# Building the head stacks of two attention layers on the chip, without a copy in DRAM

## The reference, cut to what matters

```python
x = x + tanh(g_xattn[0]) * L0_xattn(layernorm(x), ctx)     # X: 8 heads of 64
x = x + tanh(g_ffn[0])   * L0_ffn(layernorm(x))            # F: 16 heads of 8, and experts
x = x + tanh(g_xattn[1]) * L1_xattn(layernorm(x), ctx)     # B (keys and values: K): 16 heads of 8
x = x + tanh(g_ffn[1])   * L1_ffn(layernorm(x))            # C: experts
# in F and B, for each head:
attn = einsum('bhqd,bhkd->bhqk', q, k) / sqrt(8)
out  = einsum('bhqk,bhkd->bqhd', softmax(attn), v)
```

## Time and profile before

| what | value |
|---|---|
| median of 3 runs | 926.0 us (921.73 to 927.47) |
| profiled execution, span | 931.0 us; the profile gives no time around it |
| PE busy | 764.6 us, 82% of the span |
| DVE / ACT / POOL busy | 634.9 / 353.3 / 299.8 us |
| mean granted clock of PE | 0.861 of full speed |
| DRAM read / written | 22.99 / 17.10 MB |

### The profile page before, as it was taken

The page is one execution under the profiler, slowest core; times in us unless marked ns, Lnnn a source line. Parts: engine busy times, 40 slices in busy tenths (PEclk is TensorE's granted clock), DMA queues, the critical chain, the costliest instruction groups (busy, mean ns, idle before and its releaser), DMA issues.

```text
span 931.0 us, 13102 instructions
## 1 busy us (share of the span) xinstructions
PE 764.6 (82%) x5120; PEld 406.8 (44%) x5120; DVE 634.9 (68%) x1216; ACT 353.3 (38%) x444; POOL 299.8 (32%) x422
## 2 busy tenths in 40 slices
PE   4679798988999779987899799978898876786583
PEld 2355564644564245532464245534463433242231
DVE  0615577898655787678787988788556786964724
ACT  1324226214535234532545244632534244263060
POOL 5043442532244014332164135322244120333033
PEclk9879799998789788996899899996889778688587
DMA  5310300400303013030403023030503043023000
GB/s 146 76 35 15 69 10 10 101 11 6 74 15 57 11 54 77 12 57 6 113 18 60 9 66 71 21 42 8 128 1 54 1 108 78 2 68 57 2 1 12
DMA packets 64734, 40.95 MB, mean 44 GB/s; under 512 B 4912, under 2 KB 62776, under 8 KB 64664
## 3 DMA queue, kind: packets, MB, share of 16 engines
q1 hardware_dynamic: 64672, 40.12, 19.8%
HBM read 22.99 MB, written 17.10 MB: 43 GB/s over the span
## 4 chain that ended last, share of the span: by engine, by line
PE 52%; DVE 22%; DMA 12%; SPq 6%; ACT 4%; issue 2%; POOL 2%; POOLq 0%; DVEq 0%
PE psum L564 12%; DVE mx8B L903 12%; PE psum L651 8%; PE psum L571 6%; DMA q8B<-q_dB 6%; PE psum L607 5%; PE psum L639 3%; DVE mxA L826 3%; PE psum L545 3%; PE psum L555 2%; DMA qA<-mrow_d 2%; DMA k8F<-k_dF 2%; PE psum L614 2%; PE psum L620 2%; PE psum L550 1%
## 5 line engine op out<-in xcount | busy, mean ns | idle before, releaser
L903 DVE TENSOR_REDUCE mx8B<-psum 128x2 f32<-128x1024 f32 x128 | 149.9, 1214 | 42.0 <-PE psum L620 41.8
L564 PE MATMUL psum<-qA,cTX 97*128 97x256 f32 x512 | 146.7, 438 | 15.9 <-DMA qA<-mrow_d 12.8
L717 ACT ACTIVATE probB<-psum 128x1024 f32<-128x1024 f32 x128 | 125.7, 1026 | 53.9 <-PE psum L639 53.5
L951 POOL TENSOR_TENSOR half<-probX 128x512 f32<-128x512 f32 x64 | 81.5, 1274 | 165.7 <-ACT probX L704 164.9
L564 PEld LDWEIGHTS psum<-qA,cTX 97*128 97x128 f32 x512 | 106.1, 216 | 46.0 <-issue 21.8
L704 ACT ACTIVATE probX<-psum 128x1024 f32<-128x1024 f32 x64 | 65.6, 1024 | 158.4 <-PE psum L564 158.4
L620 PE MATMUL psum<-k8B,q8B 48*128 48x512 bf16 x256 | 60.8, 476 | 58.5 <-DVE mx8B L903 27.6
L717 ACT ACTIVATE probF<-psum 128x1024 f32<-128x1024 f32 x64 | 64.5, 1025 | 105.6 <-PE psum L639 104.0
L898 DVE TENSOR_REDUCE mx8F<-psum 128x4 f32<-128x1024 f32 x64 | 77.0, 1220 | 35.8 <-PE psum L614 35.7
L834 DVE RECIPROCAL rden<-psum 128x256 f32<-128x256 f32 x32 | 56.2, 1757 | 55.7 <-PE psum L575 55.6
L826 DVE TENSOR_REDUCE mxA<-psum 128x2 f32<-128x1024 f32 x64 | 76.9, 1216 | 13.5 <-PE psum L555 13.3
(11 more groups left out here) (191 smaller groups left out, 1129.7 us busy)
## 6 DMA issues: line engine op xcount, KB each, us to landing
k8B<-k_dK SPq DMA_DIRECT2D x16, 384.0 KB, 6.1
k_dK<-partsK SPq DMA_DIRECT2D x8, 384.0 KB, 4.0
q8F<-q_dF SPq DMA_DIRECT2D x16, 192.0 KB, 4.5
k8F<-k_dF SPq DMA_DIRECT2D x16, 192.0 KB, 4.9
q8B<-q_dB SPq DMA_DIRECT2D x16, 192.0 KB, 7.4
k_dK<-partsK SPq DMA_DIRECT2D x8, 256.0 KB, 4.0
cTX<-in_ctxT SPq DMA_DIRECT2D x8, 192.0 KB, 2.4
cTK<-in_ctxT SPq DMA_DIRECT2D x8, 192.0 KB, 2.5
```

Source lines behind the costliest of these rows:

```text
L564: last = mm(ps[:, c * SEQ:(c + 1) * SEQ], cT["X"][:, c * P:(c + 1) * P], qA[:, k, :], start=True, stop=True)
L717: nc.scalar.activation(prob[s][(units * b + k) % SLOTS[s]][:], ps, ACT.Exp, scale=float(D8) ** -0.5).then_inc(done["ACT"], 1)
L903: nc.vector.tensor_reduce(mx8[s][:, t, 2 * p:2 * p + 2], ps.rearrange("p (i n) -> p i n", i=2), AX.X, ALU.max, negate=True).then_inc(drain ...
L951: link("X", engine.tensor_tensor(half[:], p[:, 0:2 * SEQ], p[:, 2 * SEQ:], ALU.add))
```

## The change

The jobs `sw` and `sr` become one job `st` (`stack_parts`), which waits for the split and for the last use of the old stack, and then copies from SBUF to SBUF: one transfer for 8 rows of a stack (one parity, one of the six pairings). A transfer reads 64 partitions (every second one) of one part and writes 8 partitions of `q8` or `k8`. F has 24 of them, K 12 and B 12. The rows of maxima go from `m2` to `q8` in four transfers of one row each, without `mw`. X's rows stay as they were. The planner gets the new jobs with .35 us for each transfer of `st` and 1.3 us for the four of `mr`, and so every engine's order is planned anew.

```diff
+Q_PART, K_PART = (0, 1, 2, 0, 1, 0), (0, 0, 0, 1, 1, 2)
...
-    p.job("SP", s, "sw", b, 0, .4 * writes, ("DVE", s, "sp", b, 0), ("SP", s, "sr", b - 1, 0))
-    p.job("SP", s, "sr", b, 0, 2.8 if s == "F" else 1.4, ("SP", s, "sw", b, 0), old)
+    p.job("SP", s, "st", b, 0, .35 * writes, ("DVE", s, "sp", b, 0), old)
...
-    p.job("SP", s, "mw", b, 0, .35, ("DVE", s, "mT8", b, 0), ("SP", s, "mr", b - 1, 0))
-    p.job("SP", s, "mr", b, 0, 1.25, ("SP", s, "mw", b, 0), ("PE", s, "e8", b - 1, units - 1))
+    p.job("SP", s, "mr", b, 0, 1.3, ("DVE", s, "mT8", b, 0), ("PE", s, "e8", b - 1, units - 1))
...
-    plan_stack(p, "F", b, 1.85, 6, ("ACT", "F", "qk", b, 0), ("PE", "F", "e8", b - 1, NPAIR - 1))
+    plan_stack(p, "F", b, 1.85, 24, ("ACT", "F", "qk", b, 0), ("PE", "F", "e8", b - 1, NPAIR - 1))
...
-    plan_stack(p, "K", b, 1.85, 3, ("ACT", "K", "kk", b, 0), ("PE", "B", "e8", b - 1, 2 * NPAIR - 1))
+    plan_stack(p, "K", b, 1.85, 12, ("ACT", "K", "kk", b, 0), ("PE", "B", "e8", b - 1, 2 * NPAIR - 1))
...
-    plan_stack(p, "B", b, 1.35, 3, ("DVE", "B", "qk", b, 0), ("PE", "B", "e8", b - 1, 2 * NPAIR - 1))
+    plan_stack(p, "B", b, 1.35, 12, ("DVE", "B", "qk", b, 0), ("PE", "B", "e8", b - 1, 2 * NPAIR - 1))
...
-            def store_parts(s, b):
...
-            def load_parts(s, b):
...
+            def stack_parts(s, b):
                 sp.wait_ge(*after(s, "split", b))
                 to = "F" if s == "F" else "B"
                 sp.wait_ge(*is_full(to, "e8", b - 1, NPAIR * KEYS[to] // SEQ - 1))
+                k0, keys = (SEQ, SEQ) if s == "F" else (0, KV)
                 for i in range(2):
+                    for j in range(6):
+                        r = 64 * i + D8 * j
+                        if s != "K":
+                            engine.dma_start(q8[s][r:r + D8], parts[s][i:P:2, Q_PART[j], 0:SEQ]).then_inc(S[s]["st"], 16)
+                        if s != "B":
+                            engine.dma_start(k8[to][r:r + D8], parts[s][i:P:2, K_PART[j], k0:k0 + keys]).then_inc(S[s]["st"], 16)
...
                 elif name == "mr":
+                    sp.wait_ge(*is_done(s, "mT8", b))
                     sp.wait_ge(*is_full(s, "e8", b - 1, NPAIR * KEYS[s] // SEQ - 1))
                     for i in range(2):
+                        for t in range(2):
+                            r = 64 * i + KROWS + t
+                            engine.dma_start(q8[s][r:r + 1], m2[s][i:H8:2, t, :]).then_inc(S[s]["mr"], 16)
```

More of the change, by code:

```diff
@@ L119, in plan_attend @@
         p.fill("DVE", 1, s, "mx8", b, k, .35, 1.25, stacked, [("DVE", s, "mT8", b - 1, 0)])
-    p.fill("DVE", 0, s, "mT8", b, 0, .25, .85, [("DVE", s, "mx8", b, maxima - 1)], [("SP", s, "mw", b - 1, 0)])
-    p.job("SP", s, "mw", b, 0, .35, ("DVE", s, "mT8", b, 0), ("SP", s, "mr", b - 1, 0))
-    p.job("SP", s, "mr", b, 0, 1.25, ("SP", s, "mw", b, 0), ("PE", s, "e8", b - 1, units - 1))
+    p.fill("DVE", 0, s, "mT8", b, 0, .25, .85, [("DVE", s, "mx8", b, maxima - 1)], [("SP", s, "mr", b - 1, 0)])
+    p.job("SP", s, "mr", b, 0, 1.3, ("DVE", s, "mT8", b, 0), ("PE", s, "e8", b - 1, units - 1))
     for k in range(units):
@@ L133, in plan_f @@
     plan_norm(p, "F", b, ("DVE", "X", "out", b, 0), [("PE", "F", "moe", b - 1, 3)])
-    p.fill("ACT", 0, "F", "qk", b, 0, 1.0, 1.95, [("DVE", "F", "ln", b, 0)], [("SP", "F", "sw", b - 1, 0)])
+    p.fill("ACT", 0, "F", "qk", b, 0, 1.0, 1.95, [("DVE", "F", "ln", b, 0)], [("SP", "F", "st", b - 1, 0)])
     plan_gate(p, "F", b, (1.2, .9, 1.1))
-    plan_stack(p, "F", b, 1.85, 6, ("ACT", "F", "qk", b, 0), ("PE", "F", "e8", b - 1, NPAIR - 1))
+    plan_stack(p, "F", b, 1.85, 24, ("ACT", "F", "qk", b, 0), ("PE", "F", "e8", b - 1, NPAIR - 1))
     p.fill("DVE", 0, "F", "v8", b, 0, .5, .43, [("DVE", "F", "ln", b, 0)], [("PE", "F", "pv8", b - 1, 3)])
@@ L140, in plan_f @@
     p.fill("DVE", 0, "F", "wb", b, 0, .45, .49, [("DVE", "F", "wT", b, 0)], [("POOL", "F", "fin", b, 0)])
-    plan_attend(p, "F", b, [("SP", "F", "sr", b, 0)], ("DVE", "F", "v8", b, 0), NPAIR,
+    plan_attend(p, "F", b, [("SP", "F", "st", b, 0)], ("DVE", "F", "v8", b, 0), NPAIR,
                 [("DVE", "F", "wb", b, 0), ("POOL", "B", "xb", b - 1, 0), ("DVE", "B", "xh", b - 1, 0)])
@@ L146, in plan_k @@
     p.job("SP", "K", "ctx", b, 0, .4, ("PE", "K", "kk", b - 1, 0), ("PE", "K", "vv", b - 1, 1))
-    p.fill("ACT", 0, "K", "kk", b, 0, 1.0, 1.4, [("SP", "K", "ctx", b, 0)], [("SP", "K", "sw", b - 1, 0)])
-    plan_stack(p, "K", b, 1.85, 3, ("ACT", "K", "kk", b, 0), ("PE", "B", "e8", b - 1, 2 * NPAIR - 1))
+    p.fill("ACT", 0, "K", "kk", b, 0, 1.0, 1.4, [("SP", "K", "ctx", b, 0)], [("SP", "K", "st", b - 1, 0)])
+    plan_stack(p, "K", b, 1.85, 12, ("ACT", "K", "kk", b, 0), ("PE", "B", "e8", b - 1, 2 * NPAIR - 1))
     for k in range(2):
@@ L608, in _ @@
                 elif name == "mx8":
-                    pe.wait_ge(*after(s, "sr", b))
+                    pe.wait_ge(*after(s, "st", b))
                     if s == "F":
@@ L616, in _ @@
                     else:
-                        pe.wait_ge(*after("K", "sr", b))
+                        pe.wait_ge(*after("K", "st", b))
                         p, t = divmod(k, QT)
@@ L705, in _ @@
                 elif name in ("qk", "kk"):
-                    act.wait_ge(*after(s, "sw", b - 1))
+                    act.wait_ge(*after(s, "st", b - 1))
                     for n, j in ((SEQ, 0), (SEQ, 1)) if s == "F" else ((KV, 1),):
@@ L820, in _ @@
                 elif name == "qk":
-                    dve.wait_ge(*after("B", "sw", b - 1))
+                    dve.wait_ge(*after("B", "st", b - 1))
                     nc.vector.tensor_scalar(parts[s][:, 0, :], ps[:, 0:SEQ], bq8[s][:, 0:1], None, ALU.add)
@@ L905, in _ @@
                 elif name == "mT8":
-                    dve.wait_ge(*after(s, "mw", b - 1))
+                    dve.wait_ge(*after(s, "mr", b - 1))
                     link(s, nc.vector.tensor_copy(m2[s][:, 0, :], ps[0:H8, 0:SEQ]))
```

44 lines of the change are left out of this document (8 added, 36 removed).

## The result

The changed kernel takes **1056.5 us** (median of 4 runs, 1054.4 to 1057.5) where the kernel before takes 923.9 (916.1 to 927.5): 1.144 times as long, 95% interval 1.137 to 1.150. The direction was forecast; the size was not: 995 us with a range to 1050.

A forecast was written before the change was run, and what follows sets the result against it. No engine is full; late transfers bound the kernel, chiefly B's stack loads. The profile's 931.0 + 63 (B) + 9 (X's row) - 1 (maxima) = 1002 us, scaled to the median 997, said as 995; range 895 to 1050.

The forecast's parts named there:

- The page's first hint: B's stack: 9.8 us from the last `e8` to first use, 7.0 covered by other work, PE standing 2.86.
- The issue of .66: On SP: each new stack transfer takes .66 us to issue, as loads writing eight 512 B runs per partition did.
- the landing of F at 17.2 us: F's stack: 24 issues of .66 plus 1.4 us to land make 17.2 us, where it took 11.2.
- the maxima at about nothing: Maxima: a store and its round trip go, four issues replace two; worth -1 us at most.
- 71 us of stands: The whole kernel: +63 for the B stack, +9 for X's row, -1 for the maxima.
- X's row: SP's queue: X's row of maxima waits behind F's 24 issues, 15.8 us against 8.4 planned; +9 us.
- +63: B's stack: PE stands about 12.7 us where it stood 3.7, +9.0 us seven times.
- The law behind the 53: Stack transfers: rate falls with partitions written, 163 GB/s into 48 carried on to 53 into 8.
- the 90 that the prediction named: Sign of being wrong: an on-chip copy into 8 partitions running at over about 90 GB/s.
- issue alone: Rival, chance .16: bytes hidden, each issue .66 us; B's stack 17.2 us, stall 5.7, 948 us by the median.
- The bound of 5 us in each of 8 elements: F's stack: upper bound on its added wait, 40 us, used only for the range; nothing was charged.
- longer stalls at a lower clock: PE: longer stalls might bring more of the .53 granted clock and lengthen products; no size given, nothing charged.

The follow-up runs named there:

- the old order: Engine order of the kernel before kept: with only the maxima moved on chip, 1.002 of before; with all of the change's on-chip transfers, 1.127.
- the two queues: The changed kernel with odd heads' stack transfers issued from ACT and even heads' from SP, half the true time planned for each queue: 1.115 of before.
- all true costs: The changed kernel with the planner told .65 us for each stack transfer and 2.7 for the maxima: 1.023 of the kernel before.
- half left out: The changed kernel without the odd heads' stack transfers, planned at half of the true time, output not the reference's: .948 of the kernel before.
- the three drawn orders: The kernel before with only the maxima on chip, planned anew, .969; with the planner's assumed hop between engines at .08, 1.010; at .06, 1.019.

## Why the prediction was right or wrong

**Right.** The page's first hint, a stack that is on the path in B. The issue of .66 (measured .65), the bytes that vanish from DRAM, the landing of F at 17.2 us (17.4), the maxima at about nothing (.2% in the old order). And the central mechanism: the cover of a transfer is what the planner believes, here 10.1 us for 10.4 believed.

**The sum: near in its stands by luck, and short by the clock.** To the profile's 931.0 us the forecast added 71 us of stands and nothing for the clock. PE did stand for 70.1 us more, but only because errors cancelled: B cost 35 us less than forecast, X's row 10 less and all other idle time 7 less; F cost 29 more, K's context 15.5 more and the maxima 6.5 more. The profile's 1054.6 us are 52.6 above the forecast's 1002, and PE's busy time, which the sum didn't touch, rose by 53.5.

**B, too dear.** The forecast was 24.2 us for the stack and a stand of 12.7 us; it was 18.1 and 54.3 / 7 = 7.8. The term that failed is the rate into 8 rows, 53 GB/s carried on from the earlier trace rows, where K's transfers moved at 68 to 74 once the first were over: K 12 x 64 KiB / 69 GB/s = 11.4 us, B the rest. So +28 us where the sum had +63. The issues of K did not stretch to over 1 us either; all 12 went out in 7.81 us. The law behind the 53 failed by more: a transfer into 8 rows by itself moved at 115 to 127 GB/s, above the 90 that the prediction named as a sign of being wrong. That F's build shows 49 GB/s, near the 53, is luck: there the issue sets it. A rival was nearer: *issue alone* had 17.2 us and a stall of 5.7 for B, and for F it is what happened.

The Trainium skill ("SBUF — State Buffer", "Door 1: The DMA port swizzle") gives about 27 GB/s to a port, of which 8 rows reach two, an estimate of 54 together; the trace, with 115 and 127 for a transfer by itself, doesn't agree, and the measurement decides. What the same page says under "Can I just issue two DMAs to hit both halves?", that transfers into different halves serialize, agrees with the two queues for K: 68 GB/s as before.

**F, the wait put at nothing.** The sentence "Waits on F were 3.5 us in all, so most of this is slack; I charge nothing" was wrong: F's wait rose by 28.8 us. The 3.3 us between landing and first use were taken for slack of the work; by the planner's own rule they were the plan's. A planner that deals each engine's jobs out by their believed start puts the first use right behind the believed landing, so the slack that a trace shows is re-dealt. 17.4 us real against 10.4 believed is 7 us, and the four waits of after average 8.1. That the plan sets it is shown in part only: with the true cost planned for F alone its wait falls to 17.9 us, with all true costs to 14.8, not to the 3.5 of before. The bound of 5 us in each of 8 elements, named for the range, was the better centre.

**SP's queue, right mechanism and wrong passenger.** X's row lost nothing (-.8 us); K's context load, named as one of those "needed later" and priced at nothing, lost 15.5 us behind F's 24 issues. With the plan's errors, which of the transfers queued behind a long build is the next wanted was not to be read from the trace of before; that one would be was.

**The clock, the step that the total missed.** PE's busy time rose by 53.5 us, the largest single part of the loss; the prediction named longer stalls at a lower clock, said "I have no row for how much", and charged nothing. Timeline of PE in after, one stand in X:

```profile
526.44 3.78 PE L543 MATMUL psum<-qA,cTX 97*128 97x256 f32 x8 [6.81 <-DMA qA<-mrow_d]
```

Windows of after, during that stand and behind it:

```profile
523.00:525.00 2.00, 0.00 (x0) 0.00 (x0) 0.00 (x0) 0.00 (x0) 0.00 (x0) 0.50 0.08 21
...
529.00:533.00 4.00, 4.00 (x13) 2.40 (x13) 0.00 (x0) 1.94 (x2) 1.56 (x2) 0.50 0.00 0
533.00:537.00 4.00, 4.00 (x13) 2.49 (x12) 0.00 (x0) 1.94 (x2) 1.74 (x3) 0.50 0.00 0
537.00:541.00 4.00, 4.00 (x13) 2.47 (x12) 0.00 (x0) 1.94 (x2) 1.82 (x2) 0.50 0.00 0
541.00:545.00 4.00, 4.00 (x19) 2.19 (x19) 1.01 (x1) 1.94 (x2) 1.74 (x3) 0.50 0.02 4
```

Behind a stand of 6.81 us, PE is busy throughout from 529 to 545 and still at .50. The products of X took 502 ns on the mean for 438 before. Over all 20 kernels, PE's busy time times its mean granted clock is 640 to 666 us, so a longer busy time does go with a lower clock. What lowers the clock is less clear. With true costs PE is busy for 780.5 us and with half left out for 738.3, and it stands less in both; but in the old order it stands longest of all, 262.1 us, and is busy for only 778.3. No run held the clock apart from the stands, so its share is read from the ledger and not shown by an experiment.

**The cause.** Shown: most of the loss, 12 of 14.4 points, is the planner's .35 us for transfers that take .65 (and 1.3 for the 2.7 of the maxima); the time falls step by step as the plan comes nearer, by more than the three drawn orders differ. What is left with true costs, 2.3%, is about what orders differ by; but half of the transfers left out gives 7.5 points, so the number of transfers costs too, and the plan can only hide a part. Open: why an issue of this form takes .61 us (neither stride nor size sets it, and the one-row form takes .63), why the later transfers of K and B move at 68 to 84 GB/s when one by itself moves at over 110, and what lowers PE's clock.

## What to carry to other kernels

Where a static plan fixes the order of in-order engines, its cost constants are part of the change: time one transfer of a new kind and tell the planner before judging the idea. Slack read from the trace of a planned kernel belongs to that plan and can't be spent by a change that is planned anew. Count the issues on the one queue, for they hold up everything behind them, and reckon with a slower clock behind a stand; and plan the same kernel a second time with a harmless change of a constant, to see how much an order is worth alone.

## What the runs showed of the hardware

An issue of a transfer from 64 rows of SBUF to 8 took 609 ns at the median for 32 and for 64 KiB, from neighbouring rows and from every second one. Issue times of after by line, ns min/median/max, first and last start:

```profile
L460 SPq DMA_DIRECT2D q8F<-partsF x96: 608/609/1355, 98.6 to 876.5; - x96
...
L462 SPq DMA_DIRECT2D k8B<-partsK x96: 608/609/1196, 25.4 to 971.7; - x96
```

One transfer into 8 rows by itself moved at 115 GB/s (32 KiB) and 127 (64 KiB), with the DMA engines busy for .43 and .44 of that time. K's and B's, which followed each other without a pause, moved at 68 to 84 GB/s with .57 to .64, where the load of weights into 128 rows had 1.02; for K neither a second queue nor rows in the other half of SBUF changed that (.58). F's, one at a time, used .18 on one queue and .33 on two.

The Trainium skill ("DMA: Bandwidth & Descriptors", "Why a DMA increments its semaphore by 16 and not by 1") states that a transfer uses the largest number of engines up to 16 that divides the slowest dimension of both its sides, which is 8 for 64 rows to 8; the .43 and .44 of a transfer by itself agree roughly with half of 16 engines, and no run here told this from another limit.
